# Last stage of a four-stage kernel: units in pairs, three "up" buffers, and one ring of two banks for all other products

## What is computed

```python
h = x @ Wm + bm
t = h.reshape(bs * L_ * H, HD)              # 8 heads of 32 features
logits = t @ expert_emb
w = jax.nn.softmax(logits, axis=-1)
topw, topi = jax.lax.top_k(w, K)            # the best 2 of 16 experts
hmid = jax.nn.gelu(jnp.einsum('td,edi->tei', t, W1) + b1, approximate=False)
eo = jnp.einsum('tei,eio->teo', hmid, W2) + b2
sel = jnp.take_along_axis(eo, topi[:, :, None], axis=1)
comb = (sel * topw[:, :, None]).sum(axis=1)
out = comb.reshape(bs, L_, d)
return out @ Wo + bo
```

## Time and profile before

| what | value |
|---|---|
| median of 3 runs | 3421.45 us |
| the profiled execution's own time | 3423.49 us |
| its span, first to last instruction | 3421.4 us |
| last stage, from its first DMA issue to the end | 2624.44 to 3421.4 us |
| TensorE busy in the whole span | 3071.1 us (90%) |
| ScalarE, VectorE, GpSimd busy | 2305.4, 2650.7, 2354.3 us |
| mean granted TensorE clock | 0.959 |
| GELU, line 1881 | 512 times, 1112 ns each, 539.9 us |
| up product, line 1782 | 1024 matmuls |
| down product, line 1792 | 2048 instructions |
| mean DMA rate over the span | 98 GB/s |

### The profile page before, as it was taken

The page is one execution under the profiler, slowest core; times in us unless marked ns, Lnnn a source line. Parts: engine busy times, 40 slices in busy tenths (PEclk is TensorE's granted clock), DMA queues, the critical chain, the costliest instruction groups (busy, mean ns, idle before and its releaser), DMA issues. The chain is left out here.

```text
span 3421.4 us, 39507 instructions
## 1 busy us (share of the span) xinstructions
PE 3071.1 (90%) x11504; PEld 1686.4 (49%) x11504; DVE 2650.7 (77%) x3528; ACT 2305.4 (67%) x3491; POOL 2354.3 (69%) x1680
## 2 busy tenths in 40 slices
PE   3589999999999999998889999998975799999998
PEld 1156676666666767774333443443332333333332
DVE  5989999999999996553899999999995344455443
ACT  2467676767677676664767677667742588888887
POOL 3578898888888887772688797788873244444443
PEclk7589999999999999999899999999998899999998
DMA  2034444444444444452222222222221122222222
GB/s 95 13 96 132 123 134 124 132 127 127 127 124 135 124 125 131 143 154 67 67 71 68 73 72 70 68 74 70 67 74 47 68 99 99 105 105 104 103 102 81
DMA packets 199619, 335.38 MB, mean 98 GB/s; under 512 B 21380, under 2 KB 57381, under 8 KB 199021
## 3 DMA queue, kind: packets, MB, share of 16 engines
q1 hardware_dynamic: 199404, 332.86, 31.8%
HBM read 325.69 MB, written 7.09 MB: 97 GB/s over the span
## 5 line engine op out<-in xcount | busy, mean ns | idle before, releaser
L1449 POOL TENSOR_TENSOR c_hc<-c_h,c_c_rep 128x1024 f32<-128x1024 f32 x256 | 602.9, 2359 | 196.6 <-DVE c_h L1500 139.5
L1921 POOL TENSOR_TENSOR d_acc<-d_acc,d_prod 128x512 f32<-128x512 f32 x240 | 318.6, 1327 | 471.8 <-DVE d_prod L1989 471.1
L1500 DVE TENSOR_TENSOR_SCAN c_h<-c_decay,c_carry,c_v_ps 128x512 f32<-128x512 f32 x512 | 629.0, 1264 | 0.0
L1881 ACT ACTIVATE d_hmid<-d_up,d_b 128x1024 f32<-128x1024 f32 x512 | 539.9, 1112 | 77.4 <-PE d_up L1782 76.9
L1346 ACT ACTIVATE c_decay<-c_dt,c_a_cols 128x512 f32<-128x512 f32 x512 | 359.5, 719 | 304.1 <-DVE c_h L1500 287.4
L1192 PE MATMUL c_y_ps<-c_hc,ident 128*128 128x512 f32 x1024 | 500.4, 612 | 67.6 <-POOL c_hc L1449 57.3
L710 POOL TENSOR_TENSOR ab_inner_low<-ab_inner,ab_inner_high 128x512 fp32r<-128x512 f32 x264 | 340.9, 1291 | 212.5 <-ACT ab_inner_high L577 210.6
L566 ACT ACTIVATE ab_gate_ps<-ab_gate_ps,ab_raw_d 128x512 f32<-128x512 f32 x264 | 174.4, 661 | 416.2 <-PE ab_gate_ps L411 416.2
L1989 DVE SCALAR_TENSOR_TENSOR d_prod<-d_eo,d_b,d_w_rep 128x512 f32<-128x512 f32 x240 | 180.1, 751 | 314.5 <-PE d_eo L1792 176.3
L692 POOL TENSOR_TENSOR ab_hc<-ab_h,ab_c_rep 128x512 f32<-128x512 f32 x256 | 330.5, 1291 | 72.6 <-DVE ab_h L773 64.4
L1782 PE MATMUL d_up<-d_heads,d_w 128*128 128x512 f32 x1024 | 336.3, 435 | 16.5 <-ACT d_hmid L1881 9.4
(11 more groups left out here) (240 smaller groups left out, 6536.3 us busy)
## 6 DMA issues: line engine op xcount, KB each, us to landing
ab_raw_gu<-in_b_experts SPq DMA_DIRECT2D x264, 256.0 KB, 3.4
ab_w_rep<-ab_w_scratch SPq DMA_DIRECT2D x264, 256.0 KB, 3.6
c_c_rep<-c_c_scratch SPq DMA_DIRECT2D x256, 256.0 KB, 3.1
d_w_rep<-d_w_scratch SPq DMA_DIRECT2D x256, 256.0 KB
ab_raw_d<-in_b_experts SPq DMA_DIRECT2D x264, 129.0 KB, 2.1
ab_raw_x<-in_xT SPq DMA_DIRECT2D x32, 256.0 KB, 4.8
out<-xT SPq DMA_DIRECT2D x8, 512.0 KB, 3.4
xT<-in_xT SPq DMA_DIRECT2D x1, 3072.0 KB, 12.7
```

Source lines behind the costliest of these rows:

```text
L1449: nc.gpsimd.tensor_tensor(hc[:, q % HC], h[:, q % HR], c_rep[:, q % BC].unsqueeze(1).broadcast_to([P, PAIR, CH]), ALU.mult).then_inc(hc_re ...
L1500: nc.vector.tensor_tensor_scan(out=h[:, q % HR, m, :], data0=decay[:, i % DEC, :], data1=v_ps[m][:], initial=carry[:, i:i + 1], op0=ALU.mu ...
L1881: nc.scalar.activation(hmid[:, (2 * q + r) % HM], up_ps[r][:], ACT.Gelu, bias=b1[:, e:e + 1]).then_inc(gelu_ready, 1)
L1921: nc.gpsimd.tensor_tensor(acc[:, s, g, :], acc[:, s, g, :], prod[:, q % PR, :], ALU.add).then_inc(add_ready, 1)
```

## The change

It rewrites the order and the buffers of `layer1_experts`:

- Units are done in 16 pairs. TensorE makes the four up products of a pair, with up to two small products between them, and then both down products of the pair before. Line 1782 becomes line 1835, and line 1792 becomes 1845.
- The up products have three PSUM pairs in place of two. ScalarE may be three GELUs behind TensorE.
- Every other product, whether down, small or average, takes the next bank of one ring of two. A list made when the program is built (`ring_uses`) numbers the uses, and `take` waits until the use two places earlier has been read.
- `variance` moves from unit 24 of the next chunk to pair 8 of the chunk after that.
- `hmid` has 8 slots in place of 4.
- ScalarE copies HALF out between the two GELUs of a unit, and VectorE reads heads, output projection and means out ahead of the down products of the same pair.

```diff
-    HM, UP, EO, PR, WR = 4, 2, 2, 4, 8
+    HM, UP, EO, PR, WR = 8, 3, 2, 4, 8
+    PAIRS = NU // 2
...
-    Q_OUT, Q_MEAN, Q_CENTRE, Q_SQUARE, Q_VAR, Q_SCALE = 18, 20, 21, 23, 24, 20
-    Q_HALF, Q_HIGH, Q_LOW, Q_HEAD, Q_COPY = 0, 0, 1, 4, 5
-    Q_LOGITS, Q_KEEP_LOGITS, Q_TURN, Q_MAX, Q_EXP, Q_PICK, Q_BACK, Q_KEEP_WEIGHTS = 13, 13, 15, 16, 17, 18, 26, 26
+    U_HALF, U_HEADS, U_LOGITS, U_TURN, U_VAR, U_OUT, U_MEAN, U_BACK = (1, 2), (3, 4, 5, 6), 7, 8, 8, 9, 10, 13
+    Q_SCALE, Q_EXP, Q_PICK, Q_SQUARE = 18, 17, 18, 23
...
-        eo_ps = [ctx.enter_context(nc.psum_tensor(f"d_eo{i}", [P, CH], F32)) for i in range(EO)]
-        work_ps = ctx.enter_context(nc.psum_tensor("d_work", [P, CH], F32))
-        norm_ps = ctx.enter_context(nc.psum_tensor("d_norm", [P, CH], F32))
+        ring = [ctx.enter_context(nc.psum_tensor(f"d_ring{i}", [P, CH], F32)) for i in range(2)]
...
+            def take(kind, c, i=0):
+
+                at = number[kind, c, i]
+                if at >= 2:
+                    kind, c, i = ring_uses[at - 2]
+                    if kind == "down":
+                        pe.wait_ge(prod_ready, c * NU + i + 1 + EO)
+                    elif kind == "out":
+                        pe.wait_ge(norm.z_ready, c * 2 + i + 1 + norm.FREE)
...
             def chunk(c, s, first, last):
...
+                for u in range(PAIRS):
+                    between = list(small(c, u))
+                    up(c, s, 2 * u, 0)
+                    up(c, s, 2 * u, 1)
+                    if len(between) >= 1:
+                        small_product(1 - s, *between[0])
+                    up(c, s, 2 * u + 1, 0)
+                    if len(between) == 2:
+                        small_product(1 - s, *between[1])
+                    if u != U_OUT:
+                        up(c, s, 2 * u + 1, 1)
+                    for q in (2 * u - 2, 2 * u - 1):
+                        if q >= 0:
+                            down(c, q)
+                        elif not first:
+                            down(c - 1, NU + q)
+                    if u == U_VAR and c >= 2:
+                        variance(c - 2)
+                    if u == U_OUT:
+                        up(c, s, 2 * u + 1, 1)
...
+            down(NCH - 1, NU - 2)
             down(NCH - 1, NU - 1)
+            variance(NCH - 2)
             project_out(NCH - 1, 1, 0)
             project_out(NCH - 1, 1, 1)
```

More of the change, by code:

```diff
@@ L1683, in layer1_experts, with bank @@
         out_ready = sem("out_ready")
-        norm = Norm(nc, sb, sem, norm_ps[:], k, xT)
+        norm = Norm(nc, sb, sem, k, xT)
         ROUTE, PICKS = 11, 7
         NSPLIT = 6
+        def bank(kind, c, i=0):
+            return ring[number[kind, c, i] % 2]
         block = ctx.enter_context(nc.Block())
@@ L1788, in down @@
                 e = q // GROUPS
[L1789 removed]
+                take("down", c, q)
                 pe.wait_ge(gelu_ready, c * 2 * NU + 2 * q + 2 + UP)
                 for j in range(HPG):
[L1792 removed]
+                    last = nc.tensor.matmul(bank("down", c, q)[j * DH:(j + 1) * DH, :], w2[:, e, :],
                                             hmid[:, (2 * q + j // 2) % HM, j % 2, :], start=True, stop=True)
@@ L1796, in project_out @@
             def project_out(c, s, half):
[L1797 to L1804, removed]
+                take("out", c, half)
+                pe.wait_ge(add_ready, (c + 1) * NADD)
@@ L1805, in project_out @@
                 for g in range(GROUPS):
-                    last = nc.tensor.matmul(work_ps[:], out_w[:, g, half * P:(half + 1) * P], acc[:, s, g, :],
+                    last = nc.tensor.matmul(bank("out", c, half)[:], out_w[:, g, half * P:(half + 1) * P], acc[:, s, g, :],
                                             start=(g == 0), stop=(g == GROUPS - 1))
                 last.then_inc(out_ready, 1)
-            def chunk(c, s, first, last):
[L1811 to L1830, removed]
-                        if q == Q_LOGITS:
-                            product(c + 1, 1 - s, LOGITS)
-                        if q == Q_TURN:
-                            product(c + 1, 1 - s, TURN)
-                        if q == Q_BACK:
-                            product(c + 1, 1 - s, BACK)
@@ new lines, in mean, with variance, small_product @@
+            def mean(c):
+                take("mean", c)
+                norm.mean(pe, c, bank("mean", c)[:])
+            def variance(c):
+                take("var", c)
+                norm.variance(pe, c, bank("var", c)[:])
+            def small_product(s, kind, c, i):
+                if kind == "item":
+                    product(c, s, i)
+                elif kind == "out":
+                    project_out(c, s, i)
+                else:
+                    mean(c)
+            def chunk(c, s, first, last):
+                for u in range(PAIRS):
+                    between = list(small(c, u))
[13 more added lines that the diff above has]
+                            down(c - 1, NU + q)
+                    if u == U_VAR and c >= 2:
+                        variance(c - 2)
+                    if u == U_OUT:
+                        up(c, s, 2 * u + 1, 1)
@@ L1847, in _ @@
             over_chunks(pe, NCH, chunk)
+            down(NCH - 1, NU - 2)
             down(NCH - 1, NU - 1)
+            variance(NCH - 2)
             project_out(NCH - 1, 1, 0)
             project_out(NCH - 1, 1, 1)
-            norm.mean(pe, NCH - 1)
-            norm.variance(pe, NCH - 1)
+            mean(NCH - 1)
+            variance(NCH - 1)
         @block.scalar
@@ L1871, in keep_weights @@
                 act.wait_ge(w_stored, c * 16)
-                nc.scalar.copy(w_t[:], work_ps[:]).then_inc(wt_ready, 1)
+                nc.scalar.copy(w_t[:], bank("item", c, BACK)[:]).then_inc(wt_ready, 1)
             def chunk(c, s, first, last):
@@ L1880, in chunk @@
                             act.wait_ge(down_ready, c * NU + q + 1)
-                        nc.scalar.activation(hmid[:, (2 * q + r) % HM], up_ps[r][:], ACT.Gelu,
+                        nc.scalar.activation(hmid[:, (2 * q + r) % HM],
+                                             up_ps[(2 * q + r + c * 2 * NU) % UP][:], ACT.Gelu,
                                              bias=b1[:, e:e + 1]).then_inc(gelu_ready, 1)
+                        if r == 0 and not last:
+                            for g in range(GROUPS):
+                                if q == 2 * U_HALF[g]:
+                                    high(c + 1, g)
                     if not first:
@@ L1888, in chunk @@
                         if not is_int(c, 0, 1):
-                            norm.deviation(act, c - 2)
+                            norm.deviation(act, c - 2, bank("var", c - 2)[:])
                         if not last:
@@ L1988, in weigh @@
                     out = prod[:, q % PR, :]
-                nc.vector.scalar_tensor_tensor(out=out, in0=eo_ps[q % EO][:], scalar=b2[:, e:e + 1],
+                nc.vector.scalar_tensor_tensor(out=out, in0=bank("down", c, q)[:], scalar=b2[:, e:e + 1],
                                                in1=w_rep[:, q % WR, :], op0=ALU.add, op1=ALU.mult
@@ L2065, in _ @@
             residual(NCH - 1, 1)
-            norm.centre(dve, NCH - 1)
+            norm.centre(dve, NCH - 1, bank("mean", NCH - 1)[:])
             norm.scale(dve, NCH - 1)
```

141 lines of the change are left out of this document (88 added, 53 removed).

## The result

| | before | after |
|---|---|---|
| median of the runs | 3421.97 us (3420.22 to 3425.91, 4 runs) | 3403.68 us (3400.28 to 3404.13, 4 runs) |
| profiled execution / its span | 3423.49 / 3421.4 us | 3400.28 / 3398.4 us |
| last stage, from its first transfer to the end | 796.96 us | 774.27 us |

The ratio is 0.9939, 95% interval 0.9927 to 0.995: 18 us less, where 19 were forecast. The profiled execution of after is the fastest of its runs and that of before lies 1.5 us above its median, so the stage shows more in the two profiles, 22.7 us.

What follows compares the result with a forecast made beforehand. Engines at 91.06 us a chunk would fall to 87.4, leaving transfers at 88.4 as the bound. First spread at 2670.6, seven chunks of 88.4, 87.9 and a tail of 25.1 gave 19.0 us less: 3402 us, range 3395 to 3414.

Steps and rivals of the forecast that it cites:

- engine loop: TensorE and ScalarE waiting for each other in the last stage: 91.06 us a chunk before, 87.4 forecast after.
- transfer loop: 32 spreads and the store of weights on SP's queue: 88.4 us a chunk, left as it is by the change.
- Two loops, transfers the longer one after the change: Last stage: transfers at 88.4 us a chunk exceed engines at 87.4, so the engines wait for transfers.
- rival 1: Engines stay the bound in the last stage, at 89 to 91 us a chunk: 3407 to 3414 us; chance 0.25.
- rival 2: The loop grows a little, 91.5 to 93 us a chunk, with two ring banks: 3414 to 3425 us; chance 0.11.
- rival 3: The ring ties TensorE to the transfers, so ScalarE runs dry: 94 us a chunk, 3442 us; chance 0.07.
- Rival 4: Transfers keep up, their spacing set by consumers: 87.4 us a chunk, no wait in the last, 3380 us; chance 0.05.
- The rule of the Trainium skill: Spreads: a transfer uses as many engines as divide its slowest dimension, here 4; estimated 2.26 us where rows show 2.69.
- Pair 13: Engine loop, before the transposes back: TensorE stops 3.1 us for routing on VectorE; the pair takes 7.4 us.
- Prologue: Chunk 0's 13 products on two banks: last head copy 8.5 us earlier, the chain to the first spread moving along.
- Tail: After the last weighing: 25.1 us for 26.6, as the second output half no longer waits for the first's residual.
- The sum: First spread at 2670.6, seven chunks of 88.4, 87.9 to the last weighing, then the tail: 19.0 us less, 3402 us.

Runs made afterwards that it cites:

- experiment 3: The changed kernel with the transposes back one pair later (pair 14 instead of 13), each spread still one transfer: 3404.63 us, ratio to before 0.9946.
- experiment 1: The changed kernel with each spread issued as four transfers of 32 rows instead of one: 3383.42 us, ratio to before 0.9884.
- Experiment 4: The kernel before, with only the 13 products of chunk 0 in the prologue alternating between two banks: 3413.73 us, ratio 0.9973.
- experiment 6: The changed kernel with spreads in four transfers and two up buffers instead of three: 3512.3 us, ratio to before 1.0257.
- experiment 8: The changed kernel with spreads in four transfers and a pair's small products behind its four up products: 3433.7 us, ratio to before 1.0032.
- experiment 5: The changed kernel with both spreads in four transfers and the transposes back one pair later (pair 14): 3354.07 us, ratio to before 0.9797.

## Why the prediction was right

The time, 3402 for 3403.68, the direction and the mechanism held. That the time came within 2 us is partly luck: the steps are off by up to 2 us each, and the engine loop was put too low where the transfer loop covered it. By its steps:

- **Two loops, transfers the longer one after the change.** Right as to the bound, and shown: spreads stayed at 88.34 a chunk (forecast 88.4); with four transfers each the same products were done 20 us sooner, and with a shorter engine loop alone nothing was gained. But in the steady chunks the transfers are not the longer loop: both take 88.4 (see the engine loop below), and the 20 us lie in chunks 0 to 2 and behind the start of the last. So weighings wait in pairs 4 to 7 of chunks 3 and 4, where the forecast had pairs 2 to 7 of every chunk. Rivals 1, 2 and 3 fall with that: rival 1 by experiment 3, where a shorter engine loop changes nothing; rivals 2 and 3 as no chunk settled at 91.5 or more, though chunk 2 alone took 91.8. Rival 4 falls too, as the last weighings still wait for transfers.
- **The rule of the Trainium skill** ("DMA: Bandwidth & Descriptors", "Why a DMA increments its semaphore by 16 and not by 1") agrees in kind: a transfer whose slowest dimension is 4 was the limit, and four transfers whose slowest dimension is 32 weren't. The estimate of 2.26 us a spread from that page's 27 GiB/s for an engine (section "Specifications") does not: the last weighings, which only transfers release, stand 2.6 apart. The forecast went by the rows.
- **Engine loop, 87.4.** The shape was right and one term mis-sized. By experiment 1, against the forecast: plain pairs 4.45 (4.4), pairs 1 and 2 5.76 and 5.62 (5.65 each), 3 to 6 19.2 (19.6), 7 5.7 (5.8), 8 and 9 14.4 (14.6), 10 5.9 (5.8), 11 4.95 (5.3). Pair 13 was put at 7.4; it is 7.33 where the clock stays up and 8.9 in most chunks. So the wait for routing was sized rightly, and the fall of the clock behind it, 1.6 us, was left out. That makes 88.4. The miss stayed without effect on the time, because the transfer loop is 88.4 too: the margin of 1 us on which the forecast's likeliest case rested did not exist. "The engines spend waiting for transfers" what the pairing frees was therefore right only where the engines had less to do (chunks 0, 1 and 7, and chunk 2 behind them) or had just been faster (chunk 5, behind the one chunk that kept its clock).
- **Prologue, 8.5.** It gave 10.5. The last head copy came 9.2 us earlier inside the stage (2660.97 - 2651.48, less 0.31 by which the stage began earlier). The rest lies behind it, in what the prediction called "a chain" that "moves along": the logits alone took 2.09 us for 3.56 before. The granted clock of the prologue is 0.66 for 0.59 in the stretches above. Experiment 4 shows the whole step alone: 10.7.
- **Tail, 25.1.** It took 23.9. The second output half's wait went, as forecast; beyond that the granted clock there is 0.77 for 0.63, which the forecast had no term for. The last spread's arrival sets the start of the tail: 87.90 us after the first spread of chunk 7, forecast 87.9.
- **The sum.** Inside the stage 22.7 us were gained for 19.0 forecast: 2.0 more in the prologue, 1.2 in the tail, 0.4 in the loop. The medians differ by 18.3, with the stages ahead scattering by more than this difference.
- **What was off in the experiments' expectations.** Experiments 6 and 8 cost 129 and 50 us over experiment 1, where at most 77 and 29 were put. As I read it, a pair was costed by what each engine can cover with its buffers at the start, and not by the cycle from GELU to up product and back, which repeats in every pair. That is an argument; no run tests it. Of the 129 us, the clock's fall in pair 9 is a part (experiment 6).

## What to carry to other kernels

When a change shortens the longer of two loops, work out the other loop from the places where it once ran ahead, here the shrinking gap between store and first spread: that length is the new bound, if the shortened loop falls below it. Two loops of equal length hide each other: shortening the engines' showed nothing here until the transfers' was shortened too, and then it gave 29 us. Grouping work of one kind on an engine needed one buffer more here for the engine that it feeds: the same pairing was 0.6% faster than before with three and, even with faster transfers, 2.6% slower with two. And before a longer pair is put down to a buffer, look at the granted clock in it: most of what a ring of four seemed to give was the clock.

## What was not expected of the hardware

**TensorE's clock fell in some chunks after a stop of 2.8 us, and not in others.** The granted clock in after, chunk 3 and then chunk 4, each in the stop, in the transposes back and up products behind it, in the down products, and after these (columns as above):

```profile
3004.60:3007.30 2.70, 0.00 (x0) 0.00 (x0) 2.61 (x3) 1.68 (x2) 2.00 (x2) 1.00 0.26 100
3007.39:3008.92 1.53, 1.53 (x8) 1.03 (x8) 0.00 (x0) 0.86 (x2) 0.00 (x0) 0.95 0.26 102
3008.92:3012.43 3.51, 3.51 (x18) 0.67 (x17) 0.75 (x1) 1.75 (x2) 0.51 (x1) 0.54 0.26 100
3012.43:3016.00 3.57, 3.29 (x22) 1.70 (x24) 0.75 (x1) 2.87 (x3) 2.04 (x2) 1.00 0.70 263
...
3093.00:3095.70 2.70, 0.00 (x0) 0.00 (x0) 2.60 (x3) 1.67 (x2) 2.00 (x2) 1.00 0.26 100
3095.78:3097.27 1.49, 1.49 (x8) 1.04 (x8) 0.00 (x0) 0.82 (x2) 0.00 (x0) 1.00 0.31 114
3097.27:3099.19 1.92, 1.92 (x18) 0.48 (x17) 0.62 (x1) 1.78 (x2) 0.00 (x0) 1.00 0.26 99
```

During the stop itself it was granted in full (2.4 GHz) in both. In chunk 3 it fell only when TensorE was at work again: its mean is 0.54 over the 3.51 us of the down products, nearly the lower level (1.2 GHz), and then it is 1.00 again. In chunk 4 the same stop of 2.80 us left it at 1.00. Pair 13 took 8.6 to 9.0 us with the fall (9.95 in chunk 0, where the stop was 3.83) and 7.33 without. Experiment 6 shows the same behind stops of 3.03 us, and in experiment 8 the clock fell behind two of seven stops of 1.3 us. Where the stop was removed (experiment 5) the down products behind the transposes took 1.92 us and pair 13 4.45 to 4.47 in all seven chunks that have them. What decides in which chunk it falls stays open.

**Where the clock fell, the stop cost more than its length.** Removing a 2.8 us stop shortened a steady chunk by 4.4 us: the fall of the clock accounts for 1.6 of it (8.9 - 7.33). Where the clock stayed up the pair lost 2.9 (7.33 - 4.45).
